# Second layer's entry of a four-layer graph network: VectorE's float16 low parts of x move out of the projection loop

## The chip, the cores and the metric

The kernel runs on one core of a Trainium2 chip. The metric is the device time of one launch in microseconds (us). Five engines work side by side, each through its own instruction list in order: TensorE (PE in the rows, its weight loads PEld), VectorE (DVE), ScalarE (ACT), GpSimd (POOL) and SyncE (SP), which issues the DMAs. They wait for each other by counting semaphores.

## The reference, cut to what matters

x is 2048 x 256, adj is 2048 x 2048 of zeros and ones. Four layers follow each other, each with a residual and a layer norm. The second is the one that the change touches:

```
type_sum = adj @ x
attn_a   = sigmoid(concat([type_sum, x]) @ Wa.T + ba)      (attn_b the same with Wb, bb)
h        = x @ W_sa
scores   = (h @ a_left)[:, None] + (h @ a_right)[None, :]
e        = where(adj != 0, exp(-leaky_relu(scores, 0.01)), 0)
x_a      = (e / (sum(e, axis=1) + 1e-5)) @ h
x_b      = adj @ (x @ W_gcnb) + b_gcnb
x        = layernorm(x + sigmoid(attn_a * x_a + attn_b * x_b))
```

## The kernel before, in words

Rows are cut into T = 16 tiles of 128 and B = 4 blocks of 512. A product that needs float32 accuracy is done with operands split into a high and a low part, three matmuls for one (high by high, high by low, low by high). adj stays in SBUF as 0/1, so `adj @ x` is done as two float16 matmuls, on the high part of 2048 x (`x16[:, HI]`) and on what is left of it (`x16[:, LO]`).

The second layer begins when the four engines have drained the first (L1159 on VectorE). Its order, for each engine:

- **TensorE** (from L598): 8 groups of transposes of x; 16 projected tiles of x with `wss` (`project`, L522, six matmuls each); 4 groups that spread a row of scores over all partitions (`slrow`, L619, six matmuls of 512 columns each). The PSUM bank of group n is that of group n - 4, so a group waits until ScalarE and VectorE are through with the group four before it. Then it waits for `H_ready` = 2 and starts `block1(0)`: for each of eight pairs of tiles first some aggregation (`aggregate_tiles`, L633, four matmuls for a tile: two column halves by two parts, each tile of block 0 behind `conv_lo` for its float16 low part), then `attend` (L658, 24 matmuls), which waits for that pair's edge weights (`es_lo`). AGG_TILES gives the aggregated tiles ahead of the pairs: 4, 3, 3, 2, 2, 2, and none ahead of the last two.
- **ScalarE** (from L845): the high parts: for a projected tile `vj` (L853, 128 x 1) and `H_hi` (L854, 128 x 256); for the last groups `slrow` (L857); then the last column of `H_hi` (L858) and `wi` (L860). Then, for each pair, `es_hi` (L871) and `ef` (L873) by two exponentials of `tm`. A pair's `es_hi` waits until TensorE has used the pair two before it (`e_used`).
- **VectorE** (from L1159): the low parts: for a projected tile a copy of four columns (L1170), `H_lo` out of PSUM (L1171) and then `x16[:, LO]` (L1174, "x<-x" in the rows), which reads and writes SBUF alone. After the loop the split of `wgx` into `wgs` (two instructions, L1019 and L1020), a bias, two memsets, and then, behind `H_ready` = 1 from ScalarE, the last column of `H_lo`, `dsc`, and behind `w_exp` `wi`. Then the edges: `edge_scores` (L1200 one `nb`, L1203 two `tm`) for pairs 0 and 1, `edge_low` (L1024, `es_lo`) for pairs 0 and 1, and `block1(0)`, which starts with the scores of pair 2.
- **GpSimd** (L464): `x16[:, HI]` of all 16 tiles, each with a `conv_hi`, then `wlb`.

`wgs` is read by TensorE in `neighbours` only, behind the sixth pair of a block. The third and fourth layer follow behind drains.

Of the kernel before, what the change touches and what calls it, by code (L numbers as in the profile page):

```python
# [23 lines left out]
ALU = mybir.AluOpType  # L24
# [4 lines left out]
HI, LO = 0, 1  # L29
# [24 lines left out]
def wait_from(eng, sem, value):  # L54

    if not isinstance(value, int) or value > 0:
        eng.wait_ge(sem, value)
# [13 lines left out]
def build(nc, x_in, adj_in, w0_in, b0_in, node_in, edge_in, wsa_in, asa_in, wg_in, bg_in,  # L71
# [4 lines left out]
    T = N // P  # L76
# [10 lines left out]
    XS = 2048.0  # L87
# [3 lines left out]
    G_BANK = (6, 7, 4, 5)  # L91
    AGG_TILES = (4, 3, 3, 2, 2, 2)
    AHEAD = 3
    P0_GROUPS = 2 * KD * B + T
    P1_SPLITS = KD * B + T
    P1_GROUPS = P1_SPLITS + B
# [9 lines left out]
    with ctx:  # L106
        def sb(stack, name, shape, dt=F32):
            return stack.enter_context(nc.sbuf_tensor(name, shape, dt))

        def pair(stack, name, shape, dt=F32R):  # L110
            return [sb(stack, name + n, shape, dt) for n in ("_hi", "_lo")]

        def sem(name):
            return ctx.enter_context(nc.semaphore(name))
# [3 lines left out]
        x = sb(ctx, "x", [P, T, D])  # L118
# [21 lines left out]
        def in_room(first, *shape):  # L140
            flat = room[:, first:first + int(np.prod(shape))]
            return flat.rearrange("p (a b) -> p a b", a=shape[0]) if len(shape) == 2 else flat

        wsx = in_room(0, KD, D + 4)
        wgx = in_room(KD * (D + 4), KD, D + 2)
# [43 lines left out]
        x16 = sb(lay123, "x16", [P, 2, T, D], F16)  # L189
# [9 lines left out]
        wgs = pair(lay1, "wgs", [P, KD, D + 2])  # L199
# [35 lines left out]

        G = sb(lay23, "G", [P, T + AHEAD, HID])
        lay23.close()
# [4 lines left out]
        def bank(n, cols=CB):  # L242
            return ps[:, n, 0:cols]

        def g16(t, part, c0=0, cols=HID):

            return G[:, t, :].bitcast(F16)[:, part * HID + c0:part * HID + c0 + cols]
# [30 lines left out]
        conv_hi, conv_lo = sem("conv_hi"), sem("conv_lo")  # L278
# [27 lines left out]
        def _(sp):  # L306
# [9 lines left out]
            def load_adj(t):  # L316
                for k in range(2):

                    wait_from(sp, adj_cast, 2 * (t - 1) + k + 1)
                    sp.dma_start(adjf[:, k, :], adj_in[bass.ds(t * P, P), k * HALF:(k + 1) * HALF]) \  # L320
                        .then_inc(adj_landed[k], 16)
# [16 lines left out]

            sp.wait_ge(p0_lo, P0_GROUPS)
            load_adj(0)  # L340
# [173 lines left out]
        def _(pe):  # L514
# [13 lines left out]
            pe.wait_ge(const_ready, 3)  # L528
            for n in range(P0_GROUPS):
                if n >= 4:  # L530
# [262 lines left out]
        def _(act):  # L793
# [5 lines left out]

            for n in range(P0_GROUPS):  # L800
                act.wait_ge(p0_mm, n + 1)
# [162 lines left out]
            def hidden(b, o, frm, bias, scale):  # L964
                n = b * KH + o
                act.wait_ge(h_mm, n + 1)

                run(hh[HI][:, o, :], bank(frm), ACT.Relu, bias=bias[:, o:o + 1], scale=scale)
                act.wait_ge(h_lo, 2 + n - 1)
                run(hf[:, o % 2, :], bank(frm), ACT.Relu, bias=bias[:, o:o + 1], scale=scale).then_inc(h_f, 1)  # L970

            def rows(b, to, first, width):
                for k in range(TB):
                    act.wait_ge(r_mm, b * TB + k + 1)
                    run(tile(to, b * TB + k + first), bank(2 + k % 2, width), ACT.Copy).then_inc(r_copied, 1)

            def mid(b):
                for o in range(KH):
                    hidden(b, o, o % 2, b1c, 1.0)
                rows(b, G, AHEAD, HID)  # L980

# [10 lines left out]
            for t in range(T):  # L992

                wait_from(act, c3_lo, t - AHEAD + 1)
                run(g16(t, HI), G[:, t + AHEAD, :], ACT.Copy, scale=g1[:, 2:3]).then_inc(c3_hi, 1)
            act.wait_ge(h1_done, 4)
# [15 lines left out]
        def _(dve):  # L1012
# [3 lines left out]
            tt, stt, ts = nc.vector.tensor_tensor, nc.vector.scalar_tensor_tensor, nc.vector.tensor_scalar  # L1016

            def split(full, parts):
                own.link(nc.vector.tensor_copy(parts[HI][:, :, :], full))  # L1019
                own.link(tt(parts[LO][:, :, :], full, parts[HI][:, :, :].bitcast(F32), ALU.subtract))  # L1020

            def low(to, frm, high):

                return tt(to, frm, high.bitcast(F32), ALU.subtract)  # L1024
# [20 lines left out]
            low(w0s[LO][:, :, :], w0x[:, :, :], w0s[HI][:, :, :]).then_inc(w_ready, 1)  # L1045
            for n in range(P0_GROUPS):
                dve.wait_ge(p0_hi, n + 1)
                b, f, t = n // KD % B, n % KD, n - 4 * B
# [8 lines left out]
            nc.vector.reduce_max(nst[:, 0:1], nl[:, :], AX_X).then_inc(node_max, 1)  # L1057
            dve.wait_ge(p0_lo, P0_GROUPS)
            nc.vector.reduce_max(g1[:, 0:1], smax[:, :], AX_X).then_inc(tmax_ready, 1)
# [107 lines left out]
            for n in range(2 * B, P1_SPLITS):  # L1167
                t = n - 2 * B
                dve.wait_ge(p1_hi, n + 1)
                own.link(nc.vector.tensor_copy(ex[:, t, :], ps[:, n % 4, D:D + 4]))  # L1170
                stt(H[LO][:, t, 0:D], bank(n % 4, D), vj[:, t, :], H[HI][:, t, 0:D].bitcast(F32),  # L1171
                    ALU.mult, ALU.subtract).then_inc(p1_lo, 1)
                dve.wait_ge(conv_hi, t + 1)
                stt(x16[:, LO, t, :], x[:, t, :], XS, x16[:, HI, t, :], ALU.mult, ALU.subtract) \  # L1174
                    .then_inc(conv_lo, 1)
            split(wgx, wgs)
            dve.wait_ge(bias1_landed, 48)
            own.link(tt(ex[:, :, 2:4], ex[:, :, 2:4], bab[:, :, :].to_broadcast([P, T, 2]), ALU.add))
            dve.sem_inc(ex_ready, 1)
# [6 lines left out]
            dve.wait_ge(w_exp, 1)  # L1186
            own.link(ts(wi[:, :], wi[:, :], EPS, None, ALU.mult))

            dve.wait_ge(p1_mm, P1_GROUPS)
            dve.wait_ge(p1_hi, P1_GROUPS)  # L1190

# [5 lines left out]
            def edge_scores(b, pair):  # L1197

                j0 = 2 * pair
                own.link(ts(nb[:, :, :], adjT[:, j0:j0 + 2, bass.ds(b * CB, CB)], -1.0, -FAR, ALU.add, ALU.mult))  # L1200
                wait_from(dve, ef_ready, b * PAIRS + pair + 1 - RE // 2)
                for jt in (j0, j0 + 1):
                    stt(tm[:, jt % RE, :], slrow[:, bass.ds(b * CB, CB)], ex[:, jt, 0:1], nb[:, jt % 2, :],  # L1203
                        ALU.add, ALU.max).then_inc(tm_ready, 1)

                dve.wait_ge(tm_ready, 2 * (b * PAIRS + pair + 1))

            def edge_low(b, pair):
                n, s = b * PAIRS + pair, slice(2 * pair % RE, 2 * pair % RE + 2)
                dve.wait_ge(ef_ready, n + 1)  # L1210
                wait_from(dve, e_used, n + 1 - RE // 2)
                low(es[LO][:, s, :], ef[:, s, :], es[HI][:, s, :]).then_inc(es_lo, 1)
# [29 lines left out]
            def residual(b, k):  # L1242
                n = b * TB + k
                dve.wait_ge(sig_ready, n + 1)
                own.link(tt(y[:, k % 2, :], y[:, k % 2, :], tile(x, n), ALU.add))
                moments(k % 2)
                if k:
                    normed(T + n - 1, (k - 1) % 2, tile(x, n - 1))
                if k == TB - 1:
                    normed(T + n, k % 2, tile(x, n))  # L1250
# [3 lines left out]
            def block1(b):  # L1254


                last = isinstance(b, int) and b == B - 1
                for pair in range(2, PAIRS):
                    edge_scores(b, pair)
                    if pair > 2:  # L1260
                        edge_low(b, pair - 1)
                    if not (isinstance(b, int) and b == 0) and pair - 2 < TB:
                        residual(b - 1, pair - 2)
                    if pair == 6:
                        for f in range(KD):
                            agg_low(0, b, f)
                neighbours(b)
                edge_low(b, PAIRS - 1)
                if not last:
                    edge_scores(b + 1, 0)  # L1270
                make_gates(b)
                if last:
                    for t in range(4):
                        conv_low(1, t, dsc[:, t:t + 1])
                else:
                    edge_low(b + 1, 0)
                joined(b)
                if not last:
                    edge_scores(b + 1, 1)
                    edge_low(b + 1, 1)  # L1280
# [8 lines left out]
                dve.wait_ge(adjT_landed[u], 8 * T)  # L1289
            edge_scores(0, 0)  # L1290
            edge_scores(0, 1)
            edge_low(0, 0)
            edge_low(0, 1)
            block1(0)
            with dve.Fori(1, B - 1) as b:
                own.enter(b - 1, LINKS1)
# [67 lines left out]
            with dve.Fori(1, B) as b:  # L1364
                agg_low(2, b - 1, 1)
                hidden_low(b - 1)
                rows_max(b - 1, G, AHEAD)
                agg_low(2, b, 0)
            agg_low(2, B - 1, 1)
            hidden_low(B - 1)  # L1370
            rows_max(B - 1, G, AHEAD)
            dve.wait_ge(r_maxed, T)
# [71 lines left out]
```

## Time and profile before

| | us |
|---|---|
| median of 3 runs | 870.79 (870.46 to 871.27) |
| the profiled execution, its time | 870.08 |
| its span | 868.3 |
| TensorE busy in it | 792.3 (91%) |
| VectorE busy in it | 460.1 (53%) |
| ScalarE busy in it | 334.0 (38%) |

The busy shares are means over four layers with different limits. The change touches some 30 us of the span, from 262 us (first projected tile on VectorE) to 300 us (third pair of block 0), so the views to read are the ones that show single instructions in that stretch, engine by engine, with the idle time ahead of each and what ended it. Starts count from the start of the span. An instruction's time can overlap the next one's start, since engines take up the next while the last one is still writing: the distance from start to start is what a queue of instructions costs.

### The profile page before, as it was taken

Reading aid. Unit: us, or ns where it says so; the run is one execution under the profiler, and the core shown is the slowest. Engines: PE = TensorE matmul, PEld = TensorE weight load, DVE = VectorE, ACT = ScalarE, POOL = GpSimd, SP = SyncE. Lnnn points to the kernel's source line nnn. Section 1 sums busy time; section 2 is a strip of 40 time slices with the busy share of each in tenths; the row PEclk is TensorE's granted clock in tenths of the full one; section 3 lists DMA queues with packets and bytes.
Section 4 is the critical chain, followed back from the end, with each engine's and each line's share of the span. In section 5 each row is a group of like instructions: output and inputs, shape, how many; then the busy total and the mean of one; then the engine's idle time right before and its main releaser. Section 6 shows DMA issues by size and latency. Waiting matters only on the chain.

```text
span 868.3 us, 12739 instructions
## 1 busy us (share of the span) xinstructions
PE 792.3 (91%) x4264; PEld 521.0 (60%) x4264; DVE 460.1 (53%) x956; ACT 334.0 (38%) x531; POOL 113.0 (13%) x232
## 2 busy tenths in 40 slices
PE   5948899999969999999997999999998999998997
PEld 5936566666548687768683564556654455465343
DVE  4663667667757768787876347312226021111655
ACT  3455555555425445454554124313335131222200
POOL 1010111111254001010101112000000100000343
PEclk9979999999978999999999999999999999999999
DMA  4149999999920000000002000000000000000011
GB/s 127 35 105 231 215 231 227 231 232 235 190 49 1 13 1 2 1 0 0 0 0 73 7 0 1 1 0 0 0 0 25 1 1 0 0 0 1 18 36 43
DMA packets 114863, 50.61 MB, mean 58 GB/s; under 512 B 103568, under 2 KB 109840, under 8 KB 114832
## 3 DMA queue, kind: packets, MB, share of 16 engines
q1 hardware_dynamic: 114832, 50.22, 25.3%
q8 instruction: 17, 0.28, 0.1%
q14 instruction: 14, 0.11, 0.0%
HBM read 22.95 MB, written 2.10 MB: 29 GB/s over the span
## 4 chain that ended last, share of the span: by engine, by line
PE 45%; issue 24%; SPq 8%; DMA 6%; ACT 6%; DVE 6%; POOL 4%; ACTq 0%; POOLq 0%; DVEq 0%
PE ps L633 10%; PE ps L753 10%; PE ps L731 8%; PE ps L781 7%; DMA adjf<-in_adj 5%; SPq L337 5%; PE ps L762 3%; PE ps L718 3%; SPq L327 2%; PE ps L522 2%; ACT em L819 2%; POOL x L464 2%; DVE em L1076 1%; ACT adjb L814 1%; PE ps L546 1%
## 5 line engine op out<-in xcount | busy, mean ns | idle before, releaser
L633 PE MATMUL ps<-adjT,x 128*128 (+1 forms) x768 | 173.5, 380 | 7.4 <-DVE x L1285 3.8
L633 PEld LDWEIGHTS ps<-adjT,x 128*128 128x128 f16 x768 | 71.6, 98 | 92.9 <-issue 5.6
L573 PE MATMUL ps<-sup,supf 128*128 128x512 f16 x256 | 85.8, 385 | 2.8 <-DMA supf<-pl 2.8
L658 PE MATMUL ps<-H_hi,es_hi 128*128 128x258 f32 x256 | 76.4, 298 | 9.1 <-DVE es_lo L1024 6.0
L1024 DVE TENSOR_TENSOR hh_lo<-hf,hh_hi 128x512 fp32r<-128x512 f32 x32 | 22.2, 692 | 116.6 <-ACT hf L970 116.6
L753 PE MATMUL ps<-adjT,G 128*128 x384 | 83.6, 379 | 0.4 <-ACT hf L970 0.4
L562 PE MATMUL ps<-hT_hi,hst_hi 128*128 128x512 f32 x128 | 54.2, 423 | 22.6 <-DVE mx L1076 14.4
L658 PE MATMUL ps<-H_hi,es_lo 128*128 128x258 f32 x256 | 72.5, 283 | 0.0
L658 PE MATMUL ps<-H_lo,es_hi 128*128 128x258 f32 x256 | 72.3, 283 | 0.0
L575 PE MATMUL ps<-sup,supf 128*128 128x256 f16 x256 | 70.6, 276 | 0.0
L753 PEld LDWEIGHTS ps<-adjT,G 128*128 128x128 f16 x384 | 37.2, 98 | 45.4 <-issue 0.9
L871 ACT ACTIVATE es_hi<-tm 128x1024 fp32r<-128x1024 f32 x32 | 33.9, 1059 | 76.1 <-DVE tm L1203 63.2
L781 PE MATMUL ps<-x,adjT 128*128 128x512 f16 x256 | 58.1, 387 | 3.3 <-DVE x L1389 3.2
L658 PEld LDWEIGHTS ps<-H_hi,es_hi 128*128 128x128 f32 x256 | 48.4, 189 | 16.3 <-DVE es_lo L1024 10.2
L819 ACT ACTIVATE em<-em,negm 128x2048 f32<-128x2048 f32 x16 | 32.1, 2003 | 62.8 <-DVE negm L1110 62.8
L562 PE MATMUL ps<-hT_hi,hst_lo 128*128 128x512 f32 x128 | 52.6, 411 | 0.0
L562 PE MATMUL ps<-hT_lo,hst_hi 128*128 128x512 f32 x128 | 52.6, 411 | 0.0
L1024 DVE TENSOR_TENSOR es_lo<-ef,es_hi 128x1024 fp32r<-128x1024 f32 x32 | 39.2, 1225 | 20.0 <-ACT ef L873 12.8
L410 POOL TENSOR_TENSOR rstd<-mv,epsc 128x1 f32<-128x1 f32 x64 | 15.1, 236 | 259.4 <-DVE mv L1038 259.4
L658 PEld LDWEIGHTS ps<-H_lo,es_hi 128*128 128x128 f32 x256 | 48.6, 190 | 0.3
L658 PEld LDWEIGHTS ps<-H_hi,es_lo 128*128 128x128 f32 x256 | 48.4, 189 | 0.0
L1085 DVE SCALAR_TENSOR_TENSOR pl<-em,ph 128x1024 f16<-128x1024 f32 x32 | 37.8, 1222 | 18.6 <-ACT ph L824 18.6
(203 smaller groups left out, 1480.6 us busy)
## 6 DMA issues: line engine op xcount, KB each, us to landing
adjf<-in_adj SPq DMA_DIRECT2D x32, 512.0 KB, 4.7
x<-in_x SPq DMA_DIRECT2D x4, 512.0 KB, 8.2
out<-adjf SPq DMA_DIRECT2D x16, 128.0 KB, 1.7
adjf<-in_L_gnn_W SPq DMA_DIRECT2D x1, 1024.0 KB, 6.2
W1f<-in_L_gnn_W SPq DMA_DIRECT2D x1, 512.0 KB, 3.6
adjf<-in_L_gnn_W SPq DMA_DIRECT2D x1, 512.0 KB, 3.7
we<-in_L_gnn_edge_w SPq DMA_DIRECT2D x1, 256.0 KB, 3.8
w0x<-in_L_gnn_weight SPq DMA_DIRECT2D x1, 256.0 KB, 4.0
```

The lines of the kernel that those rows point to most:

```text
L337: sp.dma_start_transpose(PT(part, u), of[:, u, :]).then_inc(PT_landed[u][part], 16)
L562: ins = mm(bank(c), hst[p][:, u, k, :], hT[q][:, k, c * CB:(c + 1) * CB], start=(k == 0 and (p, q) == (HI, HI)), stop=(k == KD - 1 and p = ...
L573: ins = mm(bank(6 + u), PT(HI, u)[:, jt, :], sup[:, jt, :], start=(jt == 0), stop=False, skip_group_check=True)
L575: ins = mm(bank(6 + u, D), PT(LO, u)[:, jt, :], sup[:, jt, 0:D], start=False, stop=(jt == T - 1), skip_group_check=True)
L633: ins = mm(bank(4 + f), x16[:, part, jt, f * P:(f + 1) * P], adjT[:, jt, bass.ds(b * CB, CB)], start=(jt == 0 and part == HI), stop=(jt == ...
L658: ins = mm(bank(k, D + 2), es[p][:, jt % RE, k * P:(k + 1) * P], H[q][:, jt, :], start=(jt == 0 and (p, q) == (HI, HI)), stop=(jt == T - 1 ...
L731: ins = mm(bank(2 + k % 2, width), hh[p][:, o, k * P:(k + 1) * P], ws[q][:, o, :], start=(o == 0 and (p, q) == (HI, HI)), stop=(o == KH - ...
L753: ins = mm(bank(4 + o), g16(jt, part, o * P, P), adjT[:, jt, bass.ds(b * CB, CB)], start=(jt == 0 and part == HI), stop=(jt == T - 1 and p ...
L781: ins = mm(bank(u), adjT[:, jt, bass.ds(t * P, P)], f16[:, jt, :], start=(jt == 0), stop=(jt == T - 1))
L819: run(em[:, u, :], em[:, u, :], ACT.Exp, bias=negm[:, bass.ds(t, 1)], accum_out=Z[:, bass.ds(t, 1)]) \
L1024: return tt(to, frm, high.bitcast(F32), ALU.subtract)
L1085: stt(pl[:, u, cols], em[:, u, cols], TOP, ph[:, u, cols], ALU.mult, ALU.subtract).then_inc(p_lo, 1)
```

## The change

The 16 low parts of `x16` leave the loop over the projected tiles, and so does the split of `wgx` behind it. The first eight low parts are issued behind `wi`, ahead of the first `edge_scores`; two between the scores of pair 1 and the low part of pair 0; the last six between the low parts of pairs 0 and 1; and the split of `wgx` behind the low part of pair 1, ahead of `block1(0)`. No instruction is added or removed, and the other engines' lists stay as they are.

```
+    EARLY = 8
...
                 stt(H[LO][:, t, 0:D], bank(n % 4, D), vj[:, t, :], H[HI][:, t, 0:D].bitcast(F32),
                     ALU.mult, ALU.subtract).then_inc(p1_lo, 1)
-                dve.wait_ge(conv_hi, t + 1)
-                stt(x16[:, LO, t, :], x[:, t, :], XS, x16[:, HI, t, :], ALU.mult, ALU.subtract) \
-                    .then_inc(conv_lo, 1)
-            split(wgx, wgs)
             dve.wait_ge(bias1_landed, 48)
...
             own.link(ts(wi[:, :], wi[:, :], EPS, None, ALU.mult))
 
+            def conv_first(tiles):
+                for t in tiles:
+                    dve.wait_ge(conv_hi, t + 1)
+                    stt(x16[:, LO, t, :], x[:, t, :], XS, x16[:, HI, t, :], ALU.mult, ALU.subtract) \
+                        .then_inc(conv_lo, 1)
+
+            conv_first(range(EARLY))
             dve.wait_ge(p1_mm, P1_GROUPS)
             dve.wait_ge(p1_hi, P1_GROUPS)
...
             edge_scores(0, 0)
             edge_scores(0, 1)
+            conv_first(range(EARLY, EARLY + 2))
             edge_low(0, 0)
+            conv_first(range(EARLY + 2, T))
             edge_low(0, 1)
+            split(wgx, wgs)
             block1(0)
```

## Rows read from the trace of the kernel before

**Rows 1.** The page: busy time of each engine, and one of the costliest groups.

```profile
PE 792.3 (91%) x4264; PEld 521.0 (60%) x4264; DVE 460.1 (53%) x956; ACT 334.0 (38%) x531; POOL 113.0 (13%) x232
...
L658 PE MATMUL ps<-H_hi,es_hi 128*128 128x258 f32 x256 | 76.4, 298 | 9.1 <-DVE es_lo L1024 6.0
```

**Rows 2.** Windows: stretch, length; PE, PEld, DVE, ACT, POOL busy; granted clock, DMA.

```profile
259.30:264.90 5.60, 5.59 (x26) 5.60 (x27) 2.53 (x9) 1.95 (x7) 5.12 (x7) 0.50 0.00 0
264.90:275.00 10.10, 9.99 (x73) 9.06 (x73) 9.62 (x33) 7.81 (x25) 4.88 (x7) 0.99 0.01 2
...
281.60:287.10 5.50, 3.63 (x16) 1.48 (x16) 5.06 (x9) 3.34 (x4) 0.00 (x0) 1.00 0.15 48
287.10:300.00 12.90, 12.86 (x87) 10.12 (x88) 9.77 (x14) 4.56 (x5) 0.00 (x0) 1.00 0.01 1
```

**Rows 3.** Timeline (start, us, engine, line): one turn of VectorE's projection loop.

```profile
266.52 0.15 DVE L1170 COPY ex<-ps 128x4 f32<-128x4 f32 x1
...
267.12 0.41 DVE L1174 SCALAR_TENSOR_TENSOR x<-x 128x256 f16<-128x256 f32 x1
267.45 0.15 DVE L1170 COPY ex<-ps 128x4 f32<-128x4 f32 x1
```

**Rows 4.** Timeline, TensorE: first matmul of projected tile 9, and of slrow group 0.

```profile
268.43 0.28 PE L522 MATMUL ps<-wss_hi,xT_hi 128*128 128x260 f32 x1
...
274.82 0.47 PE L619 MATMUL ps<-xT_hi,wlb_hi 128*128 128x512 f32 x1
```

**Rows 5.** Timeline, ScalarE in the loop: two neighbouring tiles.

```profile
268.63 0.17 ACT L853 ACTIVATE vj<-ps 128x1 f32<-128x1 f32 x1
...
269.35 0.17 ACT L853 ACTIVATE vj<-ps 128x1 f32<-128x1 f32 x1
```

**Rows 6.** Timeline, VectorE behind the loop; in brackets idle time and releaser.

```profile
279.48 0.07 DVE L1181 MEMSET H_lo<- 128x16 f32 x1
281.40 0.19 DVE L1024 TENSOR_TENSOR H_lo<-vj,H_hi 128x16 fp32r<-128x16 f32 x1 [1.85 <-ACT H_hi L858]
...
281.79 0.43 DVE L1200 TENSOR_SCALAR nb<-adjT 128x1024 bf16<-128x1024 bf16 x1
...
284.16 1.42 DVE L1203 SCALAR_TENSOR_TENSOR tm<-slrow,ex,nb 128x512 f32<-128x512 f32 x2
285.86 1.23 DVE L1024 TENSOR_TENSOR es_lo<-ef,es_hi 128x1024 fp32r<-128x1024 f32 x1 [0.29 <-ACT ef L873]
```

**Rows 7.** Timeline, TensorE: aggregation and first attends of block 0.

```profile
281.65 3.63 PE L633 MATMUL ps<-adjT,x 128*128 128x512 bf16 x16 [1.10 <-DVE H_lo L1024]
287.14 0.39 PE L658 MATMUL ps<-H_hi,es_hi 128*128 128x258 f32 x1 [1.87 <-DVE es_lo L1024]
...
290.15 2.76 PE L633 MATMUL ps<-adjT,x 128*128 128x512 bf16 x12
292.57 0.47 PE L658 MATMUL ps<-H_hi,es_hi 128*128 128x258 f32 x1
```

**Rows 8.** Timeline, VectorE: first half of the split; three like low parts for layer 4.

```profile
277.74 0.42 DVE L1019 CAST wgs_hi<-adjf 128x516 fp32r<-128x516 f32 x1
...
531.64 1.06 DVE L1285 SCALAR_TENSOR_TENSOR x<-x 128x256 f16<-128x256 f32 x3
```

**Rows 9.** Timeline, ScalarE: exponentials of pair 0 and of pair 3.

```profile
284.72 1.04 ACT L873 ACTIVATE ef<-tm 128x1024 f32<-128x1024 f32 x1
...
295.90 1.06 ACT L871 ACTIVATE es_hi<-tm 128x1024 fp32r<-128x1024 f32 x1 [3.16 <-DVE tm L1203]
```

**Rows 10.** Timeline, TensorE: its first matmuls behind two longer idle times elsewhere.

```profile
240.20 0.38 PE L573 MATMUL ps<-sup,supf 128*128 128x512 f16 x1 [2.80 <-DMA supf<-pl]
...
663.71 8.55 PE L762 MATMUL ps<-adjT,G 128*128 128x512 bf16 x31 [4.18 <-DVE G L1377]
```

**Rows 11.** Windows: granted clock (third number from the end) behind those two.

```profile
241.00:244.40 3.40, 3.40 (x14) 1.58 (x12) 0.32 (x1) 0.00 (x0) 0.00 (x0) 0.52 0.59 114
...
664.30:667.60 3.30, 3.30 (x10) 1.17 (x8) 3.30 (x5) 2.77 (x5) 1.05 (x1) 0.52 0.00 1
```

## The prediction

> **What bounds the kernel now.** I read the page first. TensorE is busy for 91% of the span and VectorE for 53% [rows 1]: in the mean TensorE is the bound, so a VectorE edit counts only where TensorE waits for it. Of the 9.1 us that TensorE's attends wait, 6.0 go to `es_lo`. Then the windows around the edit [rows 2]. In 264.90 to 275.00 VectorE is busy 9.62 of 10.10 us and TensorE 9.99, but TensorE's figure is padded by spread-out matmuls; the timeline tells who sets the pace. In 281.60 to 287.10 TensorE works 3.63 of 5.50 us while VectorE is nearly full: here VectorE and the edge weights are the bound. From 287.10 on TensorE is full (12.86 of 12.90 us). So three stretches: the projection loop, the way from its end to the first attend at 287.14, and the rest of the layer, which follows TensorE. Whatever shifts the first attend shifts the end, unless VectorE falls behind once more.
>
> **The loop, with the 16 low parts taken out.** A turn of VectorE's loop is 0.93 us from L1170 to L1170, of which 0.33 is the step from L1174 to the next L1170; without it a turn is 0.60 [rows 3]. ScalarE's own turn is 0.72, seen where it has work waiting [rows 5]. TensorE's six matmuls take the same 0.72: 0.12 each at the high clock. So VectorE is the slowest of the three now and would be the fastest after. TensorE starts tile 9 at 268.43 and, seven tiles later, the first slrow group at 274.82 [rows 4]: 6.39 us, where 7 x 0.72 = 5.04 would do. Gain 1.35 us. Four banks give a tile 2.88 us until its bank is wanted again; from its first matmul it needs about 0.72 + 0.67 on ScalarE + 0.68 on VectorE + some 0.35 of hand-overs = 2.4 us, so the pace of 0.72 holds. Bounds of this term: 0 (something else holds TensorE) to -1.5. The earlier tiles ran at the low clock, where TensorE is slower than VectorE, and give nothing.
>
> Everything up to `H_ready` moves by the same 1.35: the slrow groups are TensorE's own, and ScalarE's L858 follows the last. VectorE already stood idle there, 1.85 us between L1181 and L1024 [rows 6]. The split taken from in front of that wait therefore saves nothing: it only lengthens the idle time, by itself and by the low parts. VectorE will wait from about 275.7 to 280.05 with nothing to do, since the first eight low parts are queued behind `H_ready`, `dsc` and `wi`.
>
> **The way to the first attend, with ten low parts put in.** The scores of pair 0 started at 281.79, 0.39 behind the start of L1024 [rows 6]. Now at that place, 281.79 - 1.35 = 280.44, stand eight low parts. Price of one in a queue: three of the same form take 1.06 us, the last 0.41 of it, so (1.06 - 0.41) / 2 = 0.325 apart [rows 8], as the 0.33 of [rows 3]. I take 0.33; the upper bound is their full 0.41. Eight are 2.64, and the scores start at 283.08. Two more, 0.66, come between the scores of pair 1 and the low part of pair 0. There VectorE waited 0.29 for `ef` [rows 6]; `ef` follows the scores by the same distance as before [rows 9], so the two low parts cover that wait. Sum at the first attend:
>
> -1.35 (loop) + 2.64 + 0.66 - 0.29 = +1.66, and with 0.04 for an own wait +1.7 us: 287.14 becomes 288.84.
>
> By the Trainium skill, "VectorE: DVE Perf Modes", section "The DRAIN you can't avoid", the next operation doesn't start before the pipe of the one in front has emptied. By that rule ten low parts would cost 10 x 0.41 = 4.1 and the sum would be +2.5; the rows above show 0.325, and I go by them.
>
> **What TensorE does in the meantime.** Its 16 aggregating matmuls took 3.63 us [rows 7] and need only tiles 0 to 3, whose low parts come every 0.33 us against 0.91 for TensorE's four matmuls. They start when the first is written, at 280.9, and end at 284.5. Then TensorE waits until 288.84: 4.3 us, where it waited 1.87 [rows 7]. That is a new danger. After an idle time of 2.80 us, and after one of 4.18, its granted clock was low (1.2 GHz, 0.52 in the window) for 3.4 us from about where it took up work [rows 10, 11]; before 287.14, after 1.87 us, it stayed high [rows 2]. So I expect it to fall. Price: at the low clock 26 matmuls of this size took 5.59 us, 0.215 each [rows 2], where they cost 0.12. In 3.3 us it does 15 that would have taken 1.8: 1.5 us lost. Bounds: 0 (stays high, or low only while idle) and 2.5 (26 x 0.095, the length of 259.30 to 264.90).
>
> The Trainium skill, "TensorE: Matmul & The Clock Gate", section "Terms", puts the penalty at the throttled time times the share of pulses withheld, here one half: 1.7 us for 3.4 us by the page, and a sum of +3.4. These f32 matmuls lost a little less than half in the rows, and I keep 1.5.
>
> **Behind the first attend.** It is to end 3.2 later than 290.15. VectorE then has, from 288.7: six low parts (2.0), the low part of pair 1 (to 291.9), the split (0.42 for its first half [rows 8], at most 1.23 for the second, a subtraction on half of the columns of L1024), the scores of pairs 2 and 3 at 1.9 each ((285.58 - 281.79) / 2 [rows 6]), and the low part of pair 2, done at about 298.8 at the latest. TensorE wants pair 1 2.42 us behind the end of attend 0 [rows 7], at 295.7, and pair 2 5.5 later, at 301.2. With the clock high these are 294.2 and 299.7, still later. So the six low parts and the split cost nothing; the cover is TensorE's own work, at least 0.9 us more than needed, and pair 2 would be late first. From pair 3 on ScalarE waits for `e_used` again (295.90, just behind attend 1 [rows 9]), and all follows TensorE. The low parts of tiles 4 to 15 are done by 290.7, before TensorE aggregates any of them. SP's and GpSimd's lists don't change; the weight load behind `H_ready` starts 1.35 earlier with nobody waiting for it. GpSimd is done with the high parts before VectorE asks.
>
> Sum: +1.7 + 1.5 = +3.2 us on the profiled execution's 870.08 (span 868.3), or 873.3. The median of the runs lies 0.7 above that execution, so the time for the median is 870.8 + 3.2 = 874.0.
>
> **Rivals.**
> - The clock holds, or is low only while TensorE idles: +1.7, 872.5. For it: where the fall lies against the work differs between cases. Against it: 2.80 us were enough.
> - The low clock lasts longer over the attends, as in 259.30 to 264.90: 1.7 + 2.5 = +4.2, 875.0. The same time comes out at +0.8 for slower low parts together with a full low stretch.
> - No change: the lateness is made up, because TensorE's other waits for `es_lo` (6.0 in all, 1.9 of it here [rows 1, 7]) shrink when its clock or its start slips: 870.8. Against it: those waits follow TensorE's own progress through `e_used`.
> - Faster: the eight low parts run in VectorE's idle time in front of `H_ready`. That decides at one point, the first attend: only 0.66 of low parts would then stand in the way, -1.35 - 0.29 + 0.66 = -1.0, 869.8. It holds only if VectorE's list reached them before ScalarE's L858; they stand behind that wait, so the trace of before speaks against it. It would need the first attend to have been bound by something other than VectorE's queue.
>
> **How the numbers follow.** Forecast 0.50; clock holds 0.20; longer low 0.12; no change 0.11; faster 0.07. A difference of 0.2% (1.7 us) is about what measurement can tell from none. The clock-holds case sits on that edge, so 0.08 of it counts as same: faster 0.07, same 0.19, slower 0.74. The range 871.2 to 876.0 leaves out the faster case and most of no change.
>
> **What would show it.** In the profile after: slrow group 0 at about 273.5; L1024 of `H_lo` near 280.05 after some 4.3 us idle on VectorE; eight low parts 0.33 apart; first attend near 288.8 with 4.3 us idle ahead of it; a granted clock of 0.5 for some 3.4 us behind it; the third pair's attend without a wait. The prediction is wrong if the first attend isn't later than 287.14, if the clock behind it stays at 1.0, or if a second wait for `es_lo` of more than 0.5 us appears in block 0.

## The result and the profile after

| | median us | runs |
|---|---|---|
| kernel before, beside the changed one | 871.02 (868.98 to 874.3) | 22 |
| changed kernel | 873.54 (870.95 to 876.53) | 22 |
| ratio | 1.0029, 95% interval 1.0019 to 1.0038 | |
| changed kernel, profiled execution | 873.0, span 871.2 | 1 |

The change made the kernel slower by 2.5 us (871 x 0.0019 to 871 x 0.0038: 1.7 to 3.3). The forecast was +3.2, and 874.0 for the median.

The page of the changed kernel: busy times as before [rows 1], and 2.6 us more of waiting for `es_lo` in the attends.

```profile
PE 792.5 (91%) x4264; PEld 521.1 (60%) x4264; DVE 461.1 (53%) x956; ACT 333.9 (38%) x531; POOL 114.2 (13%) x232
...
L659 PE MATMUL ps<-H_hi,es_hi 128*128 128x258 f32 x256 | 77.0, 301 | 11.6 <-DVE es_lo L1025 8.6
```

The timeline of VectorE in the changed kernel, which answers to [rows 6] (columns: start, us, engine, line; in brackets idle time and its releaser).

```profile
275.13 0.07 DVE L1178 MEMSET H_lo<- 128x16 f32 x1
279.55 0.19 DVE L1025 TENSOR_TENSOR H_lo<-vj,H_hi 128x16 fp32r<-128x16 f32 x1 [4.35 <-ACT H_hi L859]
...
279.93 2.77 DVE L1189 SCALAR_TENSOR_TENSOR x<-x 128x256 f16<-128x256 f32 x8
282.62 0.42 DVE L1204 TENSOR_SCALAR nb<-adjT 128x1024 bf16<-128x1024 bf16 x1
...
286.43 0.76 DVE L1189 SCALAR_TENSOR_TENSOR x<-x 128x256 f16<-128x256 f32 x2
287.11 1.22 DVE L1025 TENSOR_TENSOR es_lo<-ef,es_hi 128x1024 fp32r<-128x1024 f32 x1
288.24 2.09 DVE L1189 SCALAR_TENSOR_TENSOR x<-x 128x256 f16<-128x256 f32 x6
290.25 1.22 DVE L1025 TENSOR_TENSOR es_lo<-ef,es_hi 128x1024 fp32r<-128x1024 f32 x1
291.39 0.42 DVE L1020 CAST wgs_hi<-adjf 128x516 fp32r<-128x516 f32 x1
```

VectorE idles for 4.35 us (1.85 before) and then runs, one after the other, the eight low parts and the scores. From the start of `H_lo`'s column to that of pair 0's low part it is now 7.56 us, and it was 4.46 before: ten low parts more, less the wait of 0.29 for `ef`.

TensorE in the changed kernel, which answers to [rows 7].

```profile
280.50 3.61 PE L634 MATMUL ps<-adjT,x 128*128 128x512 bf16 x16 [1.81 <-DVE x L1189]
288.38 0.40 PE L659 MATMUL ps<-H_hi,es_hi 128*128 128x258 f32 x1 [4.27 <-DVE es_lo L1025]
...
292.88 2.76 PE L634 MATMUL ps<-adjT,x 128*128 128x512 bf16 x12
295.29 0.47 PE L659 MATMUL ps<-H_hi,es_hi 128*128 128x258 f32 x1
```

The first attend waits 4.27 us instead of 1.87, and takes 292.88 - 288.38 = 4.50 us instead of 3.01. The second starts right behind its aggregation. The windows of the changed kernel give the reason for the 4.50 (busy us of PE, PEld, DVE, ACT, POOL, then the granted clock).

```profile
284.20:288.30 4.10, 0.00 (x0) 0.00 (x0) 4.00 (x8) 3.72 (x4) 0.00 (x0) 1.00 0.00 0
288.38:291.38 3.00, 3.00 (x15) 3.00 (x16) 3.00 (x7) 0.10 (x1) 0.00 (x0) 0.54 0.02 5
295.00:305.00 10.00, 10.00 (x69) 7.80 (x68) 7.32 (x10) 4.41 (x5) 0.00 (x0) 1.00 0.00 0
```

Behind the idle time 15 of the attend's matmuls go in 3 us at a clock of 0.54, where 24 went before. Starts counted from the span's start can't be compared between the two profiles, since the stretches at the low clock in the projection loop differ too, so the text goes by distances inside the entry. From the start of `H_lo`'s column to the second aggregation (the end of attend 0) it is 290.15 - 281.40 = 8.75 us before and 292.88 - 279.55 = 13.33 after: +4.58, against 3.05 + 1.5 = 4.55 in the forecast. What follows in block 0 adds nothing and gives nothing back: the first matmul of `neighbours`, behind the sixth pair, starts at 314.98 in the kernel before and at 317.71 in the changed one, 33.58 and 38.16 us behind `H_lo`'s column, again +4.58.

```profile
314.98 0.28 PE L522 MATMUL ps<-wgs_hi,agg_hi 128*128 128x258 f32 x1
```

```profile
317.71 0.28 PE L523 MATMUL ps<-wgs_hi,agg_hi 128*128 128x258 f32 x1
```

### The profile page after: what moved, and what is told of

The parts are those of the page before. It is cut to its first block, busy times and chain, and to the rows that moved or that the text cites. A ratio compares the mean times of both kernels' runs of the same rounds, so it can differ in the third digit from the quotient of the medians.

```text
span 871.2 us, 12739 instructions
## 1 busy us (share of the span) xinstructions
PE 792.5 (91%) x4264; PEld 521.1 (60%) x4264; DVE 461.1 (53%) x956; ACT 333.9 (38%) x531; POOL 114.2 (13%) x232
## 4 chain that ended last, share of the span: by engine, by line
PE 45%; issue 26%; SPq 7%; DVE 7%; DMA 6%; ACT 4%; POOL 4%; ACTq 0%; POOLq 0%; DVEq 0%
PE ps L634 10%; PE ps L754 10%; PE ps L732 8%; PE ps L782 6%; DMA adjf<-in_adj 5%; SPq L338 3%; PE ps L763 3%; PE ps L719 3%; SPq L328 2%; PE ps L523 2%; DVE em L1077 2%; POOL x L465 1%; PE ps L547 1%; ACT ph L825 1%; POOL rstd L412 1%
## 5 line engine op out<-in xcount | busy, mean ns | idle before, releaser
L426 POOL TENSOR_TENSOR xb<-x,brow 128x256 f32<-128x256 f32 x32 | 23.4, 733 | 185.7 <-DVE y L1097 149.2
```

## The experiments

Every ratio is against runs of the kernel before on the same chip; its median differs between chips (869.2 to 871.5), so medians of different chips are not compared. Two distances are read in each profile: the **loop**, from the first projected matmul to the first slrow group, and the **entry**, from `H_lo`'s column to the end of attend 0 (attend 0 is the attend of pair 0). In brackets stand the loop's slow matmuls: its one unbroken run, early in the loop, in which matmuls follow each other by 0.21 or 0.22 us instead of 0.12.

| kernel | loop us (slow matmuls) | entry us | idle ahead of attend 0 | clock behind it |
|---|---|---|---|---|
| before, four profiles | 15.51 (24), 14.66 (15), 14.49 (15), 14.47 (15) | 8.75, 9.94, 8.73, 8.73 | 1.86 to 1.87 | falls in the second |
| changed, two profiles | 13.10 (15), 14.11 (24) | 13.33, 13.33 | 4.27, 4.26 | falls in both |
| e1 fillers | 14.20 (24) | 12.08 | 1.25 | holds |
| e2 eight in the idle time | 13.10 (15) | 10.54 | 2.28 | falls |
| e3 cover undone | 13.10 (15) | 13.32 | 4.27 | falls |
| e4 all hidden | 13.10 (15) | 8.72 | 1.86 | holds |
| e6 two ahead | 14.10 (24) | 11.67 | none; 2.51 inside the aggregation | falls behind the 2.51 |
| e7 five ahead | 13.10 (15) | 12.19 | 3.26 | falls |
| e8 fourteen ahead | 14.17 (25) | 16.04 | 6.27 | falls |
| e9 mask ahead | 12.08 (0) | 8.27 | 1.41 | holds |

**e1: fillers in TensorE's idle time.**

```
+                    if pair == 0 and isinstance(b, int):
+                        for k in range(14):
+                            mm(bank(6), x16[:, HI, k % 4, 0:P], adjT[:, k % 4, 0:CB], start=True, stop=True,
+                               skip_group_check=True)
                     attend(b, pair)
```

> The changed kernel, with 14 more matmuls of 512 columns (some 3.2 us at the high clock) that TensorE writes to an unused bank between its first 16 aggregating matmuls and the first attend; their result is not read. My theory (the low clock is a term of its own, 1.5 us): the idle time ahead of the first attend shrinks from 4.3 to about 1.1 us, the granted clock stays at 1.0 behind it, the attend of pair 0 takes 3.0 us instead of 4.5, it still starts some 4.3 us behind the last low part's place as before, and the kernel is 1.5 us faster than the changed one: +1.2 us against the kernel before (872.2 for 871.0). Rival (the clock falls for another reason than the idle time, or its fall is made up later): the time stays at +2.5 to +3. Rival (the fillers themselves delay the attend): first attend later than the low part of pair 0 allows, and slower than the changed kernel.

Measured: ratio 1.0002 (0.9989 to 1.0015), +0.2 us (-1.0 to +1.3). The timeline of TensorE in this kernel (L682 are the fillers):

```profile
283.67 3.19 PE L682 MATMUL ps<-adjT,x 128*128 128x512 bf16 x14
288.10 0.39 PE L659 MATMUL ps<-H_hi,es_hi 128*128 128x258 f32 x1 [1.25 <-DVE es_lo L1029]
291.35 2.54 PE L634 MATMUL ps<-adjT,x 128*128 128x512 bf16 x11
```

The window of its first attend:

```profile
288.10:291.10 3.00, 3.00 (x24) 2.97 (x24) 3.00 (x7) 0.10 (x1) 0.00 (x0) 1.00 0.02 5
```

More work on TensorE, and a faster kernel than the changed one: the clock holds, 24 matmuls in 3 us, and the first attend starts 8.83 us behind `H_lo`'s column in both. The entry reads 12.08 for 13.33, but the record of the first matmul of the second aggregation is missing there (11 of 12); the next two landmarks are not touched by that: attend 1 starts 5.44 us behind attend 0 (5.43 before, 6.91 in the changed kernel), and the first matmul of `neighbours` comes 36.68 us behind `H_lo`'s column for 38.16. So the fillers take 1.5 us away, and the low clock is a term of its own that goes when the idle time goes. In the runs the gain is 1.9 us against e3 below, whose entry is the changed kernel's and which ran on the same chip (medians 870.99 and 872.85), and 2.5 - 0.2 = 2.3 by the ratios; the intervals don't tell either from the 1.5 expected.

**e2: the eight low parts ahead of the wait.** The call of `conv_first(range(EARLY))` and its function move from behind `wi` to the line above `dve.wait_ge(H_ready, 1)`.

```
+            conv_first(range(EARLY))
             dve.wait_ge(H_ready, 1)
             low(H[LO][:, :, D:D + 1], vj[:, :, :], H[HI][:, :, D:D + 1]).then_inc(H_ready, 1)
...
             own.link(ts(wi[:, :], wi[:, :], EPS, None, ALU.mult))
-            conv_first(range(EARLY))
```

> The changed kernel, with its first eight low parts ahead of VectorE's wait for H_ready instead of behind wi. My theory (what costs is the place in the queue, not the instructions): the eight fill 2.7 of VectorE's 4.35 us of idle time, the first scores start 2.7 us earlier, the first attend comes 2.7 us earlier (at the end of H_lo's column plus about 6.1 us), TensorE's idle time ahead of it falls from 4.3 to about 2.3 us, and the end is 2.7 earlier, with the clock kept 4.2 earlier: -0.2 to -1.7 against the kernel before (869.3 to 870.8). Rival (the clock falls behind 2.3 us as well): the upper end of that. Rival (the lateness of the changed kernel comes from the six low parts and the split): stays above +1.5.

Measured: ratio 0.9996 (0.9983 to 1.0008), -0.3 us (-1.5 to +0.7). The timeline of VectorE in this kernel:

```profile
275.53 2.77 DVE L1171 SCALAR_TENSOR_TENSOR x<-x 128x256 f16<-128x256 f32 x8
279.77 0.19 DVE L1025 TENSOR_TENSOR H_lo<-vj,H_hi 128x16 fp32r<-128x16 f32 x1 [1.47 <-ACT H_hi L859]
```

And of TensorE, its first attend:

```profile
285.92 0.58 PE L659 MATMUL ps<-H_hi,es_hi 128*128 128x258 f32 x1 [2.28 <-DVE es_lo L1025]
```

The same instructions stand one wait further ahead, and the changed kernel's whole loss is gone (2.5 to -0.3): the attend comes 6.15 us behind `H_lo`'s column instead of 8.83. The clock fell behind 2.28 us as well (0.50 in the 3 us behind). That is the rival, which put the time at the upper end, -0.2.

**e3: the cover undone.**

```
+            split(wgx, wgs)
             dve.wait_ge(bias1_landed, 48)
...
-            conv_first(range(EARLY + 2, T))
             edge_low(0, 1)
-            split(wgx, wgs)
+            conv_first(range(EARLY + 2, T))
```

> The changed kernel, with the split of wgx back behind the loop (in front of the wait for H_ready) and the six last low parts behind the low part of pair 1 instead of in front of it. My theory (they cost nothing where they are, TensorE's work covers them): the low part of pair 1 is ready 2.0 us earlier and the scores of pair 2 start 1.2 us earlier, TensorE's attends stay where they were, the time is that of the changed kernel within 0.3 us (+2.5 against the kernel before). Rival (VectorE is late for pair 1 or 2 as well): 1 to 3 us faster than the changed kernel, and the attend of pair 1 starts closer behind the first.

Measured: ratio 1.0027 (1.0015 to 1.0039), +2.3 us; the entry is 13.32 us, 13.33 in the changed kernel. VectorE starts pair 1's low part 1.7 us sooner behind `H_lo`'s column (8.96 instead of 10.70 us, 2.0 expected) and the scores of pair 2 0.9 sooner (1.2 expected), and TensorE's attends don't move. The six low parts and the split cost nothing where the change put them, and the split's old place cost nothing either.

**e4: everything where it is covered.** As in the change, the low part leaves the loop body and the split leaves its place behind the loop; new are the places:

```
             for n in range(2 * B, P1_SPLITS):
...
+                if t < 4:
+                    conv_first((t,))
...
+            split(wgx, wgs)
+            conv_first(range(4, 13))
             dve.wait_ge(H_ready, 1)
...
             edge_low(0, 1)
+            conv_first(range(13, T))
```

> The same 16 low parts and the split, each where I expect it to cost nothing: tiles 0 to 3 in the loop (TensorE is at the low clock there and has a turn of 1.30 us), the split and tiles 4 to 12 in VectorE's idle time in front of the wait for H_ready (1.2 + 9 x 0.33 = 4.2 of 4.35 us), tiles 13 to 15 behind the low part of pair 1. My theory (the loop's gain of 1.35 is real and the rest is the first attend's delay): the first attend comes 1.35 us earlier than in the kernel before, TensorE's idle time ahead of it is 1.9 us, the clock stays high there, and the time is 1.35 us shorter: 869.6 for 871.0. Rival (freeing the loop gives nothing because something behind it absorbs it): within 0.3 of the kernel before. Rival (VectorE's own time in total is the bound of the entry): slower than the kernel before.

Measured: ratio 0.9985 (0.9974 to 0.9996), -1.3 us (-2.3 to -0.3): faster than the kernel before. The timeline of VectorE ahead of the scores:

```profile
275.28 3.11 DVE L1171 SCALAR_TENSOR_TENSOR x<-x 128x256 f16<-128x256 f32 x9
278.33 0.19 DVE L1025 TENSOR_TENSOR H_lo<-vj,H_hi 128x16 fp32r<-128x16 f32 x1
```

Nine low parts end just when `H_lo`'s column can start: no idle time on VectorE, and the column no later behind TensorE's last slrow matmul than before (278.33 - 277.16 = 1.17 us, 281.40 - 280.16 = 1.24 before). The entry is 8.72 as before, and the loop 1.4 us shorter than before at 15 slow matmuls. The loop's gain is real.

**e5, e10, e11: the kernel before again, and e12: the changed kernel again.** No edit. Each is a single execution, read for its distances and not for its time.

> The kernel before once more, for a second profile of its projection loop. In the first profile 24 of the loop's 96 matmuls ran at the low clock, in that of the changed kernel 15. From first projected matmul to first slrow group they took 15.51 and 13.10 us; the run with fillers, with 24 at the low clock, took 14.20, so at an equal clock the change gains 1.31 there. My theory: where only 15 are slow, VectorE is the slowest from an earlier tile on, and the loop before takes some 14.9 to 15.2 us, so that the change gains 1.8 to 2.1 in such executions instead of 1.35; that is why the median came out lower than forecast. Rival: the loop before takes 14.4 (13.10 + 1.31), and the gain is the same whatever the clock.

Measured: 14.66 us for the loop with 15 slow matmuls; e10 gave 14.49 and e11 14.47. Against 13.10 (15 slow) the change gains 1.4 to 1.6; with 24 slow matmuls it gains 1.3 to 1.4 (15.51 against 14.10 to 14.20). My theory of a gain of 1.8 to 2.1 falls; the rival's 14.4 was near, the gain is nearly the same whatever the clock. What this run showed instead is in the timeline of TensorE, its first attend and second aggregation:

```profile
285.93 0.39 PE L658 MATMUL ps<-H_hi,es_hi 128*128 128x258 f32 x1 [1.86 <-DVE es_lo L1024]
290.13 3.08 PE L633 MATMUL ps<-adjT,x 128*128 128x512 bf16 x12
```

The window of that attend:

```profile
285.93:288.93 3.00, 3.00 (x19) 3.00 (x20) 2.42 (x4) 0.51 (x1) 0.00 (x0) 0.74 0.02 5
```

Nearly the same idle time as in the first profile (1.86 and 1.87 us), and here the clock fell: attend 0 takes 4.20 us, and the aggregation behind it is slower too. Attend 1 starts 6.93 us behind attend 0, 5.43 in the first profile: the fall costs 1.5 us here as well, 1.2 of it in attend 0.

> The kernel before, a third profile. The second one showed the clock falling behind the 1.86 us of idle time ahead of the first attend, which the first did not. My theory now: this fall belongs to the kernel before as well, in a part of its executions, so that only a part of the 1.5 us counts as the change's. Expect the attend of pair 0 to take either 3.0 or 4.2 to 4.5 us, and the loop 15.5 (24 slow matmuls) or 14.7 (15 slow).

> The kernel before, a fourth profile, for the same count: the attend of pair 0 takes 3.0 or 4.2 to 4.5 us. If the low clock behind 1.87 us were an accident of one execution, both looks would show 3.0.

Measured: attend 0 took 288.85 - 285.86 = 2.99 and 288.20 - 285.22 = 2.98 us. So the fall shows in one of four profiles of the kernel before.

> The changed kernel, a second profile. My theory: its 4.27 us of idle time come again, and the clock falls behind them in every execution: attend of pair 0 4.4 to 4.6 us. Rival (the fall is as much a matter of chance as in the kernel before): 3.0 to 3.3.

Measured: 4.26 us of idle time, the attend 293.49 - 289.00 = 4.49 us, the entry 13.33 again. All six profiles with 2.28 us or more ahead of attend 0 in the table have a low clock behind it; of the seven with 1.87 or less one has.

**e6, e7, e8: how many low parts stand ahead of the scores.** `EARLY = 2`, `EARLY = 5`, `EARLY = 14`.

> The changed kernel with EARLY = 2: two low parts ahead of the first scores instead of eight, two between, twelve between the low parts of pairs 0 and 1. My theory: the first attend comes 6 x 0.336 = 2.0 us earlier than in the changed kernel, with 2.3 us of idle time ahead of it, after which the clock falls as it did with the eight in front of H_ready; the low part of pair 1 is done 4.0 us behind that of pair 0 plus 1.2, in time for the second attend; time 2.0 below the changed kernel, +0.5 against the kernel before. Rival (twelve low parts make pair 1 or 2 late): a new wait for es_lo of 0.5 to 2 us at the second or third attend, and +1 to +2.5.

Measured: ratio 0.9992 (0.9975 to 1.0009), -0.7 us, entry 292.26 - 280.59 = 11.67 us. The timeline of TensorE shows another place than the one expected:

```profile
281.54 1.89 PE L634 MATMUL ps<-adjT,x 128*128 128x512 bf16 x8 [1.81 <-DVE x L1189]
285.94 3.45 PE L634 MATMUL ps<-adjT,x 128*128 128x512 bf16 x8 [2.51 <-DVE x L1189]
288.83 0.78 PE L659 MATMUL ps<-H_hi,es_hi 128*128 128x258 f32 x1
```

I had overlooked that TensorE aggregates four tiles ahead of pair 0. With two low parts ready it did half of them, waited 2.51 us for tile 2, and did the rest at the low clock (0.53 from 285.94 to 288.83); that, not `es_lo`, set the first attend. So my theory was wrong on the path: the first attend comes 0.6 us earlier than in the changed kernel (8.24 us behind `H_lo`'s column instead of 8.83) and not 2.0, without idle time of its own, and most of it runs at the high clock. Together the entry is 1.66 shorter. The rival (late pairs 1 or 2) is wrong as well: both attends follow their aggregation. Whether it beats the kernel before its interval leaves open.

> The changed kernel with EARLY = 5. My theory: first attend 3 x 0.336 = 1.0 us earlier than in the changed kernel, idle time ahead of it 3.3 us, low clock behind it, +1.5 against the kernel before. Rival (TensorE's first aggregation waits for tile 5 or the clock holds): no shift of the first attend by that amount, or +0.

Measured: ratio 1.0019 (1.0003 to 1.0034), +1.7 us. Idle time 3.26; from `H_lo`'s column to the first attend 288.16 - 280.33 = 7.83 us, 1.00 less than the changed kernel's 8.83.

> The changed kernel with EARLY = 14: all low parts stand ahead of the low part of pair 0. My theory: first attend 6 x 0.336 = 2.0 us later than in the changed kernel, idle time 6.3 us ahead of it, clock low behind it for at least as long; time 2.0 above the changed kernel, +4.5 against the kernel before. Rival (late edge weights are made up later in the layer): the same as the changed kernel.

Measured: ratio 1.0057 (1.0029 to 1.0086), +5.0 us. The same distance is 292.00 - 281.16 = 10.84, 2.01 more, with 6.27 us of idle time. The windows of that idle time and of attend 0:

```profile
285.80:292.00 6.20, 0.00 (x0) 0.00 (x1) 6.01 (x11) 3.80 (x4) 0.00 (x0) 0.85 0.00 0
292.00:297.10 5.10, 5.10 (x24) 5.10 (x24) 4.80 (x8) 0.10 (x1) 0.00 (x0) 0.51 0.01 3
```

Here all but the last two of attend 0's 24 matmuls ran at the low clock: 5.2 us, 0.7 more than in the changed kernel. Low parts ahead of the scores cost 0.33 us each, in both directions. Nothing of it is made up in the block: the first matmul of `neighbours` comes 37.15 us behind `H_lo`'s column in e7 and 40.87 in e8, 1.0 less and 2.7 more (2.0 of low parts, 0.7 of clock) than the 38.16 of the changed kernel. The times go the same way (+1.7, +2.5, +5.0), though their intervals touch.

**e9: the mask of pair 0 ahead as well.** To e4 this is added (the waits for `adjT` come along from their old place, and `masked=True` makes `edge_scores` leave `nb` out):

```
-            conv_first(range(4, 13))
+            conv_first(range(4, 11))
+            for u in range(2):
+                dve.wait_ge(adjT_landed[u], 8 * T)
+            dve.wait_ge(p1_mm, P1_SPLITS)
+            dve.wait_ge(wlb_ready, 2)
+            own.link(ts(nb[:, :, :], adjT[:, 0:2, 0:CB], -1.0, -FAR, ALU.add, ALU.mult))
             dve.wait_ge(H_ready, 1)
...
-            edge_scores(0, 0)
+            edge_scores(0, 0, masked=True)
...
             edge_low(0, 1)
-            conv_first(range(13, T))
+            conv_first(range(11, T))
```

> The kernel of e4_all_hidden, in which the mask nb of pair 0 is also made in VectorE's idle time ahead of the wait for H_ready; tiles 4 to 10 stand there now (7) and tiles 11 to 15 behind the low part of pair 1. My theory (the entry is the chain H_lo, scores, exponentials, low part, first attend): from the start of H_lo's column to the first attend 5.28 instead of 5.74 us, TensorE's idle time ahead of it 1.4 instead of 1.86; 0.46 below e4_all_hidden, and up to 1 us more where the clock no longer falls: -1.6 to -2.5 against the kernel before. Rival (five low parts behind pair 1 make pair 2 late, or the idle time is full and H_lo's column itself comes later): the first attend no earlier than in e4_all_hidden, or a new wait for es_lo at the third.

Measured: ratio 0.9973 (0.9958 to 0.9988), -2.4 us (-3.7 to -1.0), the fastest of all. The timeline of VectorE:

```profile
276.80 0.42 DVE L1193 TENSOR_SCALAR nb<-adjT 128x1024 bf16<-128x1024 bf16 x1
277.61 0.19 DVE L1025 TENSOR_TENSOR H_lo<-vj,H_hi 128x16 fp32r<-128x16 f32 x1 [0.38 <-ACT H_hi L859]
...
277.99 1.42 DVE L1216 SCALAR_TENSOR_TENSOR tm<-slrow,ex,nb 128x512 f32<-128x512 f32 x2
```

And of TensorE, its first attend:

```profile
282.89 0.39 PE L659 MATMUL ps<-H_hi,es_hi 128*128 128x258 f32 x1 [1.41 <-DVE es_lo L1025]
```

The first attend comes 5.28 us behind `H_lo`'s column and 1.41 us of idle time are left; 5.28 and 1.4 were expected.

## Why the prediction was right, point by point

- **The loop** was forecast at -1.35. At an equal number of slow matmuls the chip showed -1.31 to -1.41 (24 slow) and -1.37 to -1.56 (15 slow). Every kernel with the emptied loop has 13.10 us there with 15 slow matmuls and 14.1 to 14.2 with 24 or 25 (12.08 in e9's profile, which has none), and e4, which leaves the rest of the entry as it was, turns it into -1.3 us of time. Right.
- **VectorE's idle time** ahead of `H_ready` was to be 4.3 us: 4.35. Right, and e2 shows that this is where the eight belonged.
- **Ten low parts on the way to the first attend**: 3.30 less 0.29, forecast at 0.33 each. In the profile after eight took 282.62 - 279.93 = 2.69, two 0.68; the distance from `H_lo`'s column to the attend grew from 5.74 to 8.83, 3.09 for a forecast of 3.05. A queue in which each waits until the one in front is done would have cost 4.1 for ten; eight in 2.69 don't bear that out. The Trainium skill, "VectorE: DVE Perf Modes", section "The DRAIN you can't avoid", which the prediction cites for that rule, itself excepts an operation that is not held: it starts earlier. The trace agrees with the exception: steps of 0.34 us for operations of 0.41. Right.
- **The clock** was forecast to fall, at a price of 1.5: attend 0 took 1.49 longer in the profile and, in the second, 1.48 longer than the 3.01 of the first profile of before. e1 takes the fall away by filling the idle time, and the time follows. The mechanism is right, and so is the price of one fall. What the sum had wrong is the other side: I took the kernel before to keep its clock after 1.87 us because its one profile did. It fell in one of its four profiles, where it cost 1.5 us too, so a part of the 1.5 was in the 871.02 already. An estimate with one in four: 1.5 - 0.4 = 1.1, and the sum becomes -1.4 + 3.1 + 1.1 = +2.8. The runs can't decide between the two: their interval, 1.7 to 3.3, holds the forecast's 3.2 as well as 2.8, and four profiles don't fix the share. That the forecast came out 0.7 above the measured 2.5 can be this or scatter.
- **The six low parts and the split** were costed at nothing. e3 moves them and neither the entry (13.32 for 13.33) nor the time changes. Right.
- **Rivals.** Clock holds: wrong in both profiles. Longer low stretch: not in the changed kernel, but e8 shows it at 6.27 us. No change through later waits: wrong, the 4.58 us of the entry are still there at the end of the sixth pair, and e7 and e8 move that point by -1.0 and +2.7 us. Faster: e2 is that case by design, forecast at -1.0 with the clock as before, and measured at -0.3 (-1.5 to +0.7), with a fall of the clock behind 2.28 us that the -1.0 leaves out.

## What to carry to other kernels

Moving work out of a loop pays only if its new place costs nothing: in front of a wait in which the engine idles anyway, or where another engine's work covers it, as six low parts and the split were covered behind the first attend. Here one wait decided between +2.5 us and -0.3; with the pieces sized to the idle time it was -1.3, and with the mask moved there too -2.4. Ask of each moved instruction what stands idle at the new place and what is queued behind it; in this entry the scores were, and through them TensorE's wait for its first attend. When an edit lengthens an idle time of TensorE, count the clock behind it as a second cost, and look at more than one profile of the kernel before for whether it is paid already.

## What the runs showed of the hardware that was not expected

The granted clock is not a fixed property of a kernel's timeline. At the same place, with the same 1.86 to 1.87 us of idle time ahead of it, TensorE worked at 2.4 GHz in three profiles of the kernel before (granted clock 1.00 over 3 us) and at 1.2 GHz for part of attend 0 in one (0.74 over 3 us). In the projection loop 15 matmuls were slow in eight of the fourteen profiles, 24 or 25 in five, and in e9's none. The idle time ahead of the loop went with it: 3.26 or 3.27 us ahead of all five with the most slow matmuls, 3.02 to 3.13 ahead of the eight with 15, and 3.15 ahead of e9's; which of them is the cause isn't shown. With the loop emptied, 24 slow matmuls cost 1.0 us more than 15 (14.11 against 13.10), and a fall ahead of the first attend costs 1.5. Together that is 2.5 us of the 5.3 between the lowest and the highest of the 22 runs of the kernel before; how much of the spread is due to it isn't shown. And 14 matmuls of which nothing is read made the changed kernel faster by about 2 us, as they kept TensorE at work ahead of its attends.
